# Attention's input norm computed beside the layer norm's own factor, and one product instead of two

## The chip, the cores and the metric

The kernel runs on one core of a Trainium2 chip. The metric is the device time of one execution in microseconds (us). A core has a matrix engine (TensorE, PE in the profile, with PEld for its weight loads), a vector engine (DVE), a scalar engine (ACT), GpSimd (POOL) and SyncE (SP), whose queue (SPq) issues the DMAs here. The engines run in parallel, each its own instructions in order, and meet only at semaphores.

## The reference, cut to what matters

The input is 2048 tokens of 128 channels. Six blocks follow one another, each behind a layer norm: mixture of experts, RWKV, mixture of experts, quantised feed-forward, attention of 16 heads of 64, quantised feed-forward. The change lies between the fourth block and the fifth:

```python
def _layernorm(x, axis=-1, eps=1e-05):
    m = jnp.mean(x, axis=axis, keepdims=True)
    v = jnp.var(x, axis=axis, keepdims=True)
    return (x - m) / jnp.sqrt(v + eps)

def rms_norm(x, gamma):                      # first step of the attention
    eps = 1e-12
    norm = jnp.maximum(jnp.linalg.norm(x, axis=-1, keepdims=True), eps)
    return x / norm * x.shape[-1] ** 0.5 * (gamma + 1.0)

x = x + _L1_attn_ref(_layernorm(x), ...)     # its input norm is rms_norm of the layer norm's output
```

With v the variance of a token, the layer norm's output has the length sqrt(128 v) / sqrt(v + eps). The second norm can so be had from v alone.

## The kernel before, in words

Everything stays on chip with channels on the 128 partitions and tokens along the free axis, in 4 chunks of 512 tokens (`NC`, `CH`), each of 4 tiles of 128 (`TPC`). The order of the work is written out by hand: each engine has a function for each block (`layer_norm`, `rms_norm`, `attention`, ...) and calls them one after another; semaphore counts tie the engines together. There are no planners and no pools.

A layer norm works so. PE multiplies x by a matrix of 1/128 (L575), which leaves the mean in PSUM; DVE subtracts it (L1179, into `late_cen`, which is a part of `p_raw`); ACT squares (L926). PE's `variances` (L559) multiplies each tile of squares by a column of 1/128, so that the variances of 128 tokens stand as a column, four columns a chunk. ACT takes the root of the 128x4 columns (L932, `ln_s`), DVE the reciprocal (L1184, `ln_r`). PE's `spread` (L566) takes each column, broadcast, as its weights and the identity as the other operand, which spreads the factor over all partitions. DVE multiplies the centred data by it (L1188, into `xn`, a part of `xnp`). PE runs these in the order variances 0 and 1, spread 0, variances 2, spread 1, variances 3, spread 2, spread 3.

`rms_norm` is then a second pass of the same form over `xn`: ACT squares it (L1009), PE sums (L559 again), ACT takes the root with scale 128 (L1012), DVE clamps at 1e-12 and inverts (L1355, L1356), PE spreads (L566), and DVE multiplies `xn` by the factor and by `gamma1`, which is (gamma + 1) times the root of 128 (L1360).

The attention begins with a prologue. ACT rounds `xn` to the matmul's format (L941, `x_h`), DVE takes the rest (L1194, `x_l`). When all four chunks of `x_l` are there PE projects queries and keys of heads 0 and 1 (L584 to L586, 24 matmuls) and the values of the first pair (L681 to L683). ACT and DVE evict the projections (L1032, L1371), and SP moves the pieces to where the scores want them, six DMAs a chunk and head (L352, L359). When those of head 0 have landed PE computes the scores of head 0 (L882), DVE takes their maxima (L1491), the maxima are turned and moved (L703, L1053, L328), and the main loop over 16 heads begins (L717, L718 scores, L695 next head's scores, L732 and L735 values, L1082 and L1085 exponentials, L490 their low parts on POOL).

In the weights of the prologue ACT's L1017 and L1021 and POOL's L501 and L506 make high and low parts; SP loads the second head's weights (L363) once POOL is done with the first.

Of the kernel before, what the change touches and what calls it, by code (L numbers as in the profile page):

```python
# [8 lines left out]
ACT = mybir.ActivationFunctionType  # L9
# [4 lines left out]
C = 128  # L14
T = 2048
CH = 512
NC = T // CH
NT = T // 128
TPC = CH // 128
# [9 lines left out]
RMS_EPS = 1e-12  # L29
# [38 lines left out]
def macaron_kernel(nc, a, out, g_scratch, l_scratch, r_scratch):  # L68
    ctx = ExitStack()
    with ctx:  # L70
        def sb(name, shape, dt=fp32, where=ctx):
            return where.enter_context(nc.sbuf_tensor(name, shape, dt))

        def sem(name):
            return ctx.enter_context(nc.semaphore(name))
# [4 lines left out]
        xn = xnp[:, 1:T + 1]  # L80
# [5 lines left out]
        ln_s = sb("ln_s", [128, NT])  # L86
        eps = sb("eps", [128, 1])
        ln_r = sb("ln_r", [128, NT])
        gamma1 = sb("gamma1", [C, 1])


# [76 lines left out]
        late_cen, late_sqr = low_half[:, 0:T], low_half[:, T:2 * T]  # L168
# [5 lines left out]
        ps = ctx.enter_context(nc.psum_tensor("ps", [128, 8, CH], fp32))  # L174
# [13 lines left out]
        ln_std, ln_rec, ln_bc, ln_out = sem("ln_std"), sem("ln_rec"), sem("ln_bc"), sem("ln_out")  # L188
# [8 lines left out]
        wkv_out, o_ps = sem("wkv_out"), sem("o_ps")  # L197
        f_ps, f_sigmoid, f_silu, f_prod, f_hi, f_lo, f_down = (
            sem("f_ps"), sem("f_sigmoid"), sem("f_silu"), sem("f_prod"), sem("f_hi"), sem("f_lo"), sem("f_down"))
        rms_sq, rms_sum, rms_std, rms_rec, rms_bc, rms_out = (  # L200
            sem("rms_sq"), sem("rms_sum"), sem("rms_std"), sem("rms_rec"), sem("rms_bc"), sem("rms_out"))
        qk_loaded = sem("qk_loaded")
        wv_loaded, wo_loaded = sem("wv_loaded"), sem("wo_loaded")
        qkw_hi, qkw_lo, vw_hi, vw_lo = sem("qkw_hi"), sem("qkw_lo"), sem("vw_hi"), sem("vw_lo")
# [18 lines left out]
        def chunk(c):  # L223
            return ds(c * CH, CH)
# [326 lines left out]
        def _(pe):  # L551
            mm = nc.tensor.matmul

            def variances(src_ready, count, done, c, sqr):

                pe.wait_ge(src_ready, count)
                for t in range(TPC):
                    tile = slice(c * CH + t * 128, c * CH + t * 128 + 128)
                    last = mm(ps[:, 4 + c, t:t + 1], sqr[:, tile], inv_c[:, 0:1], start=True, stop=True)  # L559
                last.then_inc(done, 1)  # L560

            def spread(src_ready, count, done, c):

                pe.wait_ge(src_ready, count)
                for t in range(TPC):
                    last = mm(ps[:, c, t * 128:t * 128 + 128],  # L566
                              ln_r[:, TPC * c + t:TPC * c + t + 1].to_broadcast([128, 128]), ident[:, :], start=True, stop=True)
                last.then_inc(done, 1)
# [90 lines left out]
                    down(c - 1)  # L659
                down(NC - 1)  # L660

            def rms_norm():
                for c in range(NC + 1):
                    if c < NC:
                        variances(rms_sq, c + 1, rms_sum, c, late_sqr)
                    if c > 0:
                        spread(rms_rec, c, rms_bc, c - 1)

            def project_qk(par, c, bank):

                w_hi_ = qk_h[par][:, :, :].rearrange("p a d -> p (a d)")
# [238 lines left out]
            layer_norm(3)  # L910
            quant_ffn(0, 3)
            layer_norm(4)
            rms_norm()
            attention()
            layer_norm(5)
            quant_ffn(1, 5)
# [3 lines left out]
        def _(act):  # L920
            af = nc.scalar.activation

            def layer_norm(k):
                for c in range(NC):
                    act.wait_ge(ln_cen, NC * k + c + 1)
                    af((sqr if k < 3 else late_sqr)[:, chunk(c)], (cen if k < 3 else late_cen)[:, chunk(c)],  # L926
                       ACT.Square).then_inc(ln_sq, 1)
                if k == 0:
                    act.wait_ge(const_ready, CONST)
                for c in range(NC):  # L930
                    act.wait_ge(ln_var, NC * k + c + 1)
                    af(ln_s[:, TPC * c:TPC * c + TPC], ps[:, 4 + c, 0:TPC], ACT.Sqrt, bias=eps[:, 0:1]).then_inc(ln_std, 1)  # L932

            def high_parts(j):

                for c in range(NC):
                    if j == 3:
                        act.wait_ge(rms_out, c + 1)
                    else:
                        act.wait_ge(ln_out, NC * (0, 2, 3, 0, 5)[j] + c + 1)  # L940
                    af(x_h[:, chunk(c)], xn[:, chunk(c)], ACT.Copy).then_inc(xh_done, 1)  # L941

            def split_weights():
# [49 lines left out]
            def quant_ffn(k):  # L993
                high_parts(2 * k + 2)
                for c in range(NC):
# [5 lines left out]
                    for ht in range(HT1):  # L1001
                        act.wait_ge(f_prod, PRIME + at * HT1 + ht + 1)
                        act.wait_ge(f_down, PRIME + at)
                        af(f_h[:, ht, :], f_hid[:, ht, :], ACT.Copy).then_inc(f_hi, 1)

            def rms_norm():
                for c in range(NC):
                    act.wait_ge(ln_out, NC * 4 + c + 1)
                    af(late_sqr[:, chunk(c)], xn[:, chunk(c)], ACT.Square).then_inc(rms_sq, 1)  # L1009
                for c in range(NC):  # L1010
                    act.wait_ge(rms_sum, c + 1)
                    af(ln_s[:, TPC * c:TPC * c + TPC], ps[:, 4 + c, 0:TPC], ACT.Sqrt, scale=float(C)).then_inc(rms_std, 1)  # L1012

            def high_qk_weights(par, head):

# [135 lines left out]
            layer_norm(3)  # L1151
            quant_ffn(0)
            layer_norm(4)
            rms_norm()
            attention()
            layer_norm(5)
            quant_ffn(1)
# [3 lines left out]
        def _(dve):  # L1161
# [7 lines left out]
            def step(ins):  # L1169

                steps[0] += 1
                ins.then_inc(dve_step, 1)
                dve.wait_ge(dve_step, steps[0])

            def layer_norm(k):
                centred = cen if k < 3 else late_cen
                for c in range(NC):
                    dve.wait_ge(ln_mean, NC * k + c + 1)
                    tt(centred[:, chunk(c)], x[:, chunk(c)], ps[:, c, :], ALU.subtract).then_inc(ln_cen, 1)  # L1179
                for c in range(NC + 1):  # L1180
                    if c < NC:
                        tiles = slice(TPC * c, TPC * c + TPC)
                        dve.wait_ge(ln_std, NC * k + c + 1)
                        nc.vector.reciprocal(ln_r[:, tiles], ln_s[:, tiles]).then_inc(ln_rec, 1)  # L1184
                    if c > 0:
                        dve.wait_ge(ln_bc, NC * k + c)
                        dve.wait_ge(ln_cen, NC * k + c)
                        tt(xn[:, chunk(c - 1)], centred[:, chunk(c - 1)], ps[:, c - 1, :], ALU.mult).then_inc(ln_out, 1)  # L1188

            def low_parts(j):  # L1190

# [136 lines left out]
            def quant_ffn(k):  # L1328
# [16 lines left out]
                    if c > 0:  # L1345
                        add_down(c - 1)
                add_down(NC - 1)

            def rms_norm():

                for c in range(NC + 1):
                    if c < NC:
                        tiles = slice(TPC * c, TPC * c + TPC)
                        dve.wait_ge(rms_std, c + 1)
                        step(ts(ln_s[:, tiles], ln_s[:, tiles], RMS_EPS, None, ALU.max))  # L1355
                        nc.vector.reciprocal(ln_r[:, tiles], ln_s[:, tiles]).then_inc(rms_rec, 1)  # L1356
                    if c > 0:
                        done = chunk(c - 1)
                        dve.wait_ge(rms_bc, c)
                        stt(xn[:, done], xn[:, done], gamma1[:, 0:1], ps[:, c - 1, :], ALU.mult, ALU.mult).then_inc(rms_out, 1)  # L1360

            def low_qk(head, par, n, bank, hi, lo, staged):

# [157 lines left out]
            step(ts(gamma1[:, :], gamma1[:, :], 1.0, float(C) ** 0.5, ALU.add, ALU.mult))  # L1521
            quant_ffn(0)
            layer_norm(4)
            rms_norm()
            attention()
            layer_norm(5)
            quant_ffn(1)
# [39 lines left out]
```

## Time and profile before

| | us |
|---|---|
| median of 3 runs | 2193.35 (2187.97 to 2199.1) |
| the profiled execution | 2188.44 |
| its span, first to last instruction | 2186.7 |
| PE busy in the span | 2024.6 (93%) |
| DVE busy | 1846.7 (84%) |
| ACT busy | 1524.8 (70%) |
| POOL busy | 1416.0 (65%) |
| mean granted clock of PE | 0.950 of full speed |

A busy share is an average over stages with different limits. The layer norm ahead of the attention and the second norm lie between 578.8 and 607.7 us, the prologue of the attention from there to 672 us, its main loop from 672 to about 2,136 us. In the rows below a time is counted from the start of the span, "[idle before <-releaser]" is how long the engine stood before that row and what ended it, and rows with xN are N instructions merged.

### The profile page before, as it was taken

The numbers are of one execution on the slowest core, as the hardware profiler recorded it, in microseconds if no ns is written. First come the engines' busy times: TensorE is split into PE (matmuls) and PEld (weight loads), VectorE is DVE, ScalarE is ACT, GpSimd is POOL, SyncE is SP. The second block draws the span as 40 slices with busy tenths as digits, with TensorE's granted clock in tenths as the row PEclk, the third lists the DMA queues.
The fourth block names the chain that finished last, engine by engine and source line by source line (L and its number), as shares of the span: only waits on it lengthen the run. The fifth ranks groups of instructions, "written<-read, shape, count | busy, mean of one in ns | idle before, by whom it ended". The sixth has DMA issues, their size and how long they took to land. (4 is left out here: it accounts for less than half of the span.)

```text
span 2186.7 us, 25774 instructions
## 1 busy us (share of the span) xinstructions
PE 2024.6 (93%) x8352; PEld 1443.5 (66%) x8352; DVE 1846.7 (84%) x1997; ACT 1524.8 (70%) x1877; POOL 1416.0 (65%) x660
## 2 busy tenths in 40 slices
PE   5999738999868999999999999999999999999887
PEld 4777527777645766767676676676667667666554
DVE  5888785887567899899889889989988998999785
ACT  4666425665425788788788778878878787887764
POOL 1000010000206899899999989989999998999882
PEclk7999857999878999999999999999999999999998
DMA  3310002110050123032130322303223131220000
GB/s 106 75 49 30 0 0 55 49 52 17 0 119 1 42 48 69 16 70 50 41 68 19 68 42 48 68 14 73 43 47 68 18 70 39 48 69 16 6 1 20
DMA packets 77272, 94.68 MB, mean 43 GB/s; under 512 B 31755, under 2 KB 35211, under 8 KB 76870
## 3 DMA queue, kind: packets, MB, share of 16 engines
q1 hardware_dynamic: 77142, 93.04, 18.6%
q8 instruction: 70, 1.15, 0.2%
q14 instruction: 60, 0.49, 0.1%
HBM read 41.11 MB, written 1.42 MB: 19 GB/s over the span
## 5 line engine op out<-in xcount | busy, mean ns | idle before, releaser
L490 POOL TENSOR_TENSOR p_l<-p_raw,p_h 128x1024 fp32r<-128x1024 f32 x512 | 1242.3, 2454 | 140.8 <-ACT p_h L1085 126.7
L1082 ACT ACTIVATE p_raw<-ps 128x1024 f32<-128x1024 f32 x512 | 567.2, 1108 | 234.7 <-PE ps L718 234.1
L1401 DVE TENSOR_REDUCE m_part<-ps 128x1 f32<-128x1024 f32 x480 | 584.5, 1218 | 125.0 <-PE ps L695 124.2
L1085 ACT ACTIVATE p_h<-ps 128x1024 fp32r<-128x1024 f32 x512 | 524.1, 1024 | 0.0
L717 PE MATMUL ps<-qa,ka 128*128 128x512 f32 x1024 | 444.8, 434 | 2.0 <-ACT m_t L1053 2.0
L718 PE MATMUL ps<-qb,kb 65*128 65x512 f32 x1024 | 408.5, 399 | 0.0
L732 PE MATMUL ps<-p_h,v_hl 128*128 128x512 f32 x1024 | 403.1, 394 | 2.3 <-POOL p_l L490 2.2
L1395 DVE TENSOR_REDUCE l_sum<-p_raw 128x128 f32<-128x1280 f32 x256 | 377.1, 1477 | 0.4
L695 PE MATMUL ps<-ka,qa 128*128 128x512 f32 x960 | 315.1, 409 | 12.7 <-DVE m_part L1401 12.3
L735 PE MATMUL ps<-p_l,v_hl 128*64 128x512 f32 x1024 | 320.8, 394 | 0.0
L1381 DVE TENSOR_REDUCE p_raw<-p_raw 128x128 f32<-128x1024 f32 x256 | 309.0, 1208 | 11.7 <-ACT p_raw L1082 11.7
L717 PEld LDWEIGHTS ps<-qa,ka 128*128 128x128 f32 x1024 | 194.8, 190 | 113.3 <-issue 72.4
L965 ACT ACTIVATE big<-ps,b 128x512 f32<-128x512 f32 x256 | 175.7, 690 | 116.3 <-PE ps L586 116.3
L732 PEld LDWEIGHTS ps<-p_h,v_hl 128*128 128x128 f32 x1024 | 193.3, 189 | 80.2 <-issue 4.6
L695 PEld LDWEIGHTS ps<-ka,qa 128*128 128x128 f32 x960 | 171.8, 190 | 91.5 <-DVE m_part L1401 58.9
L718 PEld LDWEIGHTS ps<-qb,kb 65*128 65x128 f32 x1024 | 194.8, 190 | 53.1 <-issue 16.1
L735 PEld LDWEIGHTS ps<-p_l,v_hl 128*64 128x64 f32 x1024 | 138.3, 135 | 71.3 <-issue 1.1
L1234 DVE TENSOR_TENSOR h_l<-big,h_h 128x512 fp32r<-128x512 f32 x256 | 165.6, 689 | 6.2
L465 POOL MEMSET p_raw<- 128x512 f32 x1 | 0.6, 566 | 246.9 <-DVE x L1248 246.9
L463 POOL TENSOR_TENSOR cen<-big 128x2048 f32<-128x2048 f32 x1 | 4.5, 4549 | 229.6 <-ACT big L983 229.6
L1254 DVE CAST h_h<-big 128x512 fp32r<-128x512 f32 x128 | 54.6, 427 | 66.4 <-ACT big L965 66.4
L584 PE MATMUL ps<-h_h,w_l 128*128 128x512 f32 x256 | 103.9, 406 | 0.4
(185 smaller groups left out, 2669.2 us busy)
## 6 DMA issues: line engine op xcount, KB each, us to landing
big<-g_scratch SPq DMA_DIRECT2D x64, 256.0 KB, 3.2
xnp<-r_scratch SPq DMA_DIRECT2D x59, 256.0 KB, 3.9
qa<-qk_hi SPq DMA_DIRECT2D x112, 128.0 KB, 2.3
ka<-qk_hi SPq DMA_DIRECT2D x56, 128.0 KB, 2.3
kb<-qk_hi SPq DMA_DIRECT2D x56, 128.0 KB, 2.3
ka<-xnp SPq DMA_DIRECT2D x28, 128.0 KB, 2.3
qb<-xnp SPq DMA_DIRECT2D x28, 128.0 KB, 2.4
ka<-qk_low SPq DMA_DIRECT2D x28, 128.0 KB, 3.6
```

The costliest lines, as they stand in the source:

```text
L490: nc.gpsimd.tensor_tensor(p_l[:, g % 4, :, :], slots(g), p_h[:, g % 4, :, :].bitcast(fp32), ALU.subtract).then_inc(pl_done, 1)
L695: last = mm(ps[:, 4 + b, :], qa[par][:, it * 128:it * 128 + 128], ka[par][:, chunk(2 * half + b)], start=True, stop=True)
L717: mm(st, ka[par][:, jt * 128:jt * 128 + 128], qa[par][:, ds(c * CH, CH)], start=True, stop=False)
L718: last = mm(st, kb[par][:, jt * 128:jt * 128 + 128], qb[par][:, ds(c * CH, CH)], start=False, stop=True)
L732: return mm(ps[:, bank, :], v_hl[:, par, 2 * g + j, :], p_h[:, g % 4, j, :], start=start, stop=stop)
L735: return mm(ps[0:DH, bank, :], v_hl[:, par, 2 * g + j, 0:DH], p_l[:, g % 4, j, :], start=False, stop=False)
L965: af(h_raw[:, u % 4, :], ps[:, u % 4, :], ACT.Relu, bias=b1[:, e, ht:ht + 1]).then_inc(h_relu, 1)
L1082: af(slots(g), s_t, ACT.Exp).then_inc(raw_done, 1)
L1085: af(p_h[:, g % 4, :, :], s_t, ACT.Exp).then_inc(ph_done, 1)
L1381: nc.vector.tensor_reduce(p_raw[:, ACC, cols, 0], p_raw[:, 0:ACC, cols, :].rearrange("p g n b -> p n g b"), AX.XY, ALU.add).then_inc(half_ ...
L1395: nc.vector.tensor_reduce(l_sum[:, cols], p_raw[:, ACC:GROUPS + 1, cols, :].rearrange("p g n b -> p n g b"), AX.XY, ALU.add).then_inc(all_ ...
L1401: nc.vector.tensor_reduce(m_part[:, it, half:half + 1], ps[:, 4:6, :].rearrange("p b n -> p (b n)"), AX.X, ALU.max).then_inc(s_max, 1)
```

## The change

The function `rms_norm` is gone on all three engines. ACT's `layer_norm`, for the fifth layer norm (k == 4) alone, takes a second root of the same variances, scaled by 128, into a new 128x16 tile `ln_n`. DVE's new `norm_factor` makes of the two columns one factor: r = 1/ln_s, n = ln_n r, n = max(n, 1e-12), n = 1/n, factor = r n, written to `ln_r`. Each of the first four waits for the one ahead of it through a semaphore. The layer norm's last product becomes a product with three operands, centred data, `gamma1` and the spread factor. ACT's rounding of `xn` waits for this product instead of for the second pass.

```diff
+        ln_n = sb("ln_n", [128, NT])
...
@@ tensor engine
-            def rms_norm():
-                for c in range(NC + 1):
-                    if c < NC:
-                        variances(rms_sq, c + 1, rms_sum, c, late_sqr)
-                    if c > 0:
-                        spread(rms_rec, c, rms_bc, c - 1)
...
@@ scalar engine
                 for c in range(NC):
                     act.wait_ge(ln_var, NC * k + c + 1)
                     af(ln_s[:, TPC * c:TPC * c + TPC], ps[:, 4 + c, 0:TPC], ACT.Sqrt, bias=eps[:, 0:1]).then_inc(ln_std, 1)
+                    if k == 4:
+                        af(ln_n[:, TPC * c:TPC * c + TPC], ps[:, 4 + c, 0:TPC], ACT.Sqrt, scale=float(C)).then_inc(rms_std, 1)
...
-                    if j == 3:
-                        act.wait_ge(rms_out, c + 1)
-                    else:
-                        act.wait_ge(ln_out, NC * (0, 2, 3, 0, 5)[j] + c + 1)
+                    act.wait_ge(ln_out, NC * (0, 2, 3, 4, 5)[j] + c + 1)
                     af(x_h[:, chunk(c)], xn[:, chunk(c)], ACT.Copy).then_inc(xh_done, 1)
...
-            def rms_norm():
-                for c in range(NC):
-                    act.wait_ge(ln_out, NC * 4 + c + 1)
-                    af(late_sqr[:, chunk(c)], xn[:, chunk(c)], ACT.Square).then_inc(rms_sq, 1)
-                for c in range(NC):
-                    act.wait_ge(rms_sum, c + 1)
-                    af(ln_s[:, TPC * c:TPC * c + TPC], ps[:, 4 + c, 0:TPC], ACT.Sqrt, scale=float(C)).then_inc(rms_std, 1)
...
@@ vector engine
+            def norm_factor(c, tiles):
+
+                factor, norm = ln_r[:, tiles], ln_n[:, tiles]
+                dve.wait_ge(rms_std, c + 1)
+                step(nc.vector.reciprocal(factor, ln_s[:, tiles]))
+                step(tt(norm, norm, factor, ALU.mult))
+                step(ts(norm, norm, RMS_EPS, None, ALU.max))
+                step(nc.vector.reciprocal(norm, norm))
+                tt(factor, factor, norm, ALU.mult).then_inc(ln_rec, 1)
...
                         dve.wait_ge(ln_std, NC * k + c + 1)
-                        nc.vector.reciprocal(ln_r[:, tiles], ln_s[:, tiles]).then_inc(ln_rec, 1)
+                        if k == 4:
+                            norm_factor(c, tiles)
+                        else:
+                            nc.vector.reciprocal(ln_r[:, tiles], ln_s[:, tiles]).then_inc(ln_rec, 1)
                     if c > 0:
                         dve.wait_ge(ln_bc, NC * k + c)
                         dve.wait_ge(ln_cen, NC * k + c)
-                        tt(xn[:, chunk(c - 1)], centred[:, chunk(c - 1)], ps[:, c - 1, :], ALU.mult).then_inc(ln_out, 1)
+                        if k == 4:
+                            stt(xn[:, chunk(c - 1)], centred[:, chunk(c - 1)], gamma1[:, 0:1], ps[:, c - 1, :],
+                                ALU.mult, ALU.mult).then_inc(ln_out, 1)
+                        else:
+                            tt(xn[:, chunk(c - 1)], centred[:, chunk(c - 1)], ps[:, c - 1, :], ALU.mult).then_inc(ln_out, 1)
...
-            def rms_norm():
-
-                for c in range(NC + 1):
-                    if c < NC:
-                        tiles = slice(TPC * c, TPC * c + TPC)
-                        dve.wait_ge(rms_std, c + 1)
-                        step(ts(ln_s[:, tiles], ln_s[:, tiles], RMS_EPS, None, ALU.max))
-                        nc.vector.reciprocal(ln_r[:, tiles], ln_s[:, tiles]).then_inc(rms_rec, 1)
-                    if c > 0:
-                        done = chunk(c - 1)
-                        dve.wait_ge(rms_bc, c)
-                        stt(xn[:, done], xn[:, done], gamma1[:, 0:1], ps[:, c - 1, :], ALU.mult, ALU.mult).then_inc(rms_out, 1)
```

DVE's instructions before, from the fifth layer norm's reciprocals to the low parts `x_l` (the products into `xnp` of L1188 are the layer norm's, those of L1360 the second norm's):

```order
525 L1184 RECIPROCAL ln_r<-ln_s 128x4 x2
526 L1188 TENSOR_TENSOR xnp<-p_raw,ps 128x512
529 L1184 RECIPROCAL ln_r<-ln_s 128x4
530 L1188 TENSOR_TENSOR xnp<-p_raw,ps 128x512 x2
531 L1355 TENSOR_SCALAR ln_s<-ln_s 128x4
532 L1356 RECIPROCAL ln_r<-ln_s 128x4
535 L1360 SCALAR_TENSOR_TENSOR xnp<-xnp,gamma,ps 128x512
539 L1355 TENSOR_SCALAR ln_s<-ln_s 128x4
540 L1356 RECIPROCAL ln_r<-ln_s 128x4
541 L1360 SCALAR_TENSOR_TENSOR xnp<-xnp,gamma,ps 128x512 x2
542 L1194 TENSOR_TENSOR x_l<-xnp,x_h 128x512 x4
```

And in the changed kernel, the same stretch (a middle chunk left out; the two blocks of five at its start are chunks 0 and 1):

```order
525 L1161 RECIPROCAL ln_r<-ln_s 128x4
526 L1162 TENSOR_TENSOR ln_n<-ln_n,ln_r 128x4
527 L1163 TENSOR_SCALAR ln_n<-ln_n 128x4
528 L1164 RECIPROCAL ln_n<-ln_n 128x4
529 L1165 TENSOR_TENSOR ln_r<-ln_r,ln_n 128x4
530 L1161 RECIPROCAL ln_r<-ln_s 128x4
535 L1184 SCALAR_TENSOR_TENSOR xnp<-p_raw,gamma,ps 128x512
546 L1165 TENSOR_TENSOR ln_r<-ln_r,ln_n 128x4
547 L1184 SCALAR_TENSOR_TENSOR xnp<-p_raw,gamma,ps 128x512 x2
548 L1193 TENSOR_TENSOR x_l<-xnp,x_h 128x512 x4
```

Each reciprocal of the layer norm has become five small instructions ahead of the spread that waits for them, and the second round of small instructions and products is gone.

PE before, from the means of the fifth layer norm to the first projection (32 matmuls of variances and 32 of spreads, in two rounds):

```order
1643 L575 MATMUL ps<-x,inv_c 128x512 x4
1644 L559 MATMUL ps<-inv_c,p_raw 128x1 x8
1645 L566 MATMUL ps<-ident,ln_r 128x128 x4
1646 L559 MATMUL ps<-inv_c,p_raw 128x1 x4
1647 L566 MATMUL ps<-ident,ln_r 128x128 x4
1648 L559 MATMUL ps<-inv_c,p_raw 128x1 x4
1649 L566 MATMUL ps<-ident,ln_r 128x128 x8
1650 L559 MATMUL ps<-inv_c,p_raw 128x1 x8
1651 L566 MATMUL ps<-ident,ln_r 128x128 x4
1655 L566 MATMUL ps<-ident,ln_r 128x128 x8
1656 L584 MATMUL ps<-x_h,qk_l 128x512
```

PE in the changed kernel:

```order
1647 L566 MATMUL ps<-ident,ln_r 128x128 x4
1648 L559 MATMUL ps<-inv_c,p_raw 128x1 x4
1649 L566 MATMUL ps<-ident,ln_r 128x128 x8
1650 L584 MATMUL ps<-x_h,qk_l 128x512
1651 L585 MATMUL ps<-x_h,qk_h 128x512
```

The first round is unchanged and the projections follow it directly.

## Rows read from the trace of the kernel before

**Rows 1.** The page's busy times and instruction counts over the span.
```profile
PE 2024.6 (93%) x8352; PEld 1443.5 (66%) x8352; DVE 1846.7 (84%) x1997; ACT 1524.8 (70%) x1877; POOL 1416.0 (65%) x660
```

**Rows 2.** Busy time by stretch; the columns are in the first line.
```profile
core 0: us, PE busy (x) PEld busy (x) DVE busy (x) ACT busy (x) POOL busy (x), PEclk, DMA share, GB/s
586.00:597.00 11.00, 10.77 (x53) 10.78 (x54) 3.39 (x8) 2.31 (x6) 0.00 (x0) 0.54 0.01 1
597.00:607.00 10.00, 9.86 (x60) 9.57 (x60) 3.79 (x13) 2.88 (x8) 0.00 (x0) 0.67 0.00 0
...
669.00:679.00 10.00, 7.92 (x20) 5.61 (x21) 1.23 (x1) 6.22 (x8) 2.67 (x2) 0.50 0.00 1
...
1044.00:2032.00 988.00, 978.55 (x4053) 676.82 (x4052) 902.14 (x844) 792.20 (x891) 926.19 (x418) 1.00 0.22 47
```

**Rows 3.** DVE in order of time, 586 to 611 us: start, length, instruction.
```profile
586.00 0.33 DVE L1184 RECIPROCAL ln_r<-ln_s 128x4 f32<-128x4 f32 x2 [2.27 <-ACT ln_s L932]
...
596.36 0.69 DVE L1188 TENSOR_TENSOR xnp<-p_raw,ps 128x512 f32<-128x512 f32 x1 [1.02 <-PE ps L566]
597.81 0.17 DVE L1355 TENSOR_SCALAR ln_s<-ln_s 128x4 f32<-128x4 f32 x1 [0.76 <-ACT ln_s L1012]
598.01 0.18 DVE L1356 RECIPROCAL ln_r<-ln_s 128x4 f32<-128x4 f32 x1
...
606.90 0.75 DVE L1360 SCALAR_TENSOR_TENSOR xnp<-xnp,gamma,ps 128x512 f32<-128x512 f32 x1 [0.96 <-PE ps L566]
607.57 3.01 DVE L1194 TENSOR_TENSOR x_l<-xnp,x_h 128x512 fp32r<-128x512 f32 x4
```

**Rows 4.** PE in order of time, 586 to 612 us.
```profile
586.23 1.56 PE L566 MATMUL ps<-ident,ln_r 128*128 128x128 f32 x8 [1.55 <-DVE ln_r L1184]
587.58 1.71 PE L559 MATMUL ps<-inv_c,p_raw 128*128 128x1 f32 x8
589.15 2.05 PE L566 MATMUL ps<-ident,ln_r 128*128 128x128 f32 x8
591.00 1.71 PE L559 MATMUL ps<-inv_c,p_raw 128*128 128x1 f32 x8
592.56 3.76 PE L566 MATMUL ps<-ident,ln_r 128*128 128x128 f32 x16
...
610.63 0.74 PE L584 MATMUL ps<-x_h,qk_l 128*128 128x512 f32 x1 [3.76 <-DVE x_l L1194]
```

**Rows 5.** ACT in order of time, 585 to 608 us.
```profile
585.70 0.42 ACT L932 ACTIVATE ln_s<-ps,eps 128x4 f32<-128x4 f32 x2
...
592.74 0.26 ACT L932 ACTIVATE ln_s<-ps,eps 128x4 f32<-128x4 f32 x1 [3.15 <-PE ps L559]
...
607.68 0.63 ACT L941 ACTIVATE x_h<-xnp 128x512 fp32r<-128x512 f32 x1 [1.08 <-DVE xnp L1360]
```

**Rows 6.** DVE, dependent small instructions of the first block, near 43 us.
```profile
43.28 0.25 DVE L1222 RECIPROCAL rt<-rt 128x16 f32<-128x16 f32 x1
43.57 0.18 DVE L1223 TENSOR_TENSOR rt<-rt 128x16 f32<-128x16 f32 x1
43.78 0.29 DVE L1224 TENSOR_TENSOR best<-best,rt 128x128 f32<-128x128 f32 x1
```

**Rows 7.** The prologue in order of time: ACT, POOL, SP's queue, PE.
```profile
611.76 0.46 POOL L501 TENSOR_TENSOR qk_l<-qk_raw,qk_h 128x128 fp32r<-128x128 f32 x1 [1.74 <-ACT qk_h L1017]
...
612.97 1.15 SPq L352 DMA_DIRECT2D qa<-p_raw  x2
...
628.58 0.60 SPq L359 DMA_DIRECT2D qb<-p_raw  x1
...
631.05 3.72 PE L882 MATMUL ps<-ka,qa 128*128 128x512 f32 x8 [7.71 <-DMA qb<-p_raw]
```

**Rows 8.** PE, last layer norm (2147 us) and start of the main loop (from 672 us).
```profile
2147.94 1.16 PE L566 MATMUL ps<-ident,ln_r 128*128 128x128 f32 x8 [1.55 <-DVE ln_r L1184]
2148.93 0.95 PE L559 MATMUL ps<-inv_c,p_raw 128*128 128x1 f32 x8
...
673.11 0.63 PE L717 MATMUL ps<-qa,ka 128*128 128x512 f32 x1
673.54 0.63 PE L718 MATMUL ps<-qb,kb 65*128 65x512 f32 x1
...
679.05 0.40 PE L717 MATMUL ps<-qa,ka 128*128 128x512 f32 x1
679.28 0.39 PE L718 MATMUL ps<-qb,kb 65*128 65x512 f32 x1
```

More of the change, by code:

```diff
@@ L199, in macaron_kernel @@
             sem("f_ps"), sem("f_sigmoid"), sem("f_silu"), sem("f_prod"), sem("f_hi"), sem("f_lo"), sem("f_down"))
-        rms_sq, rms_sum, rms_std, rms_rec, rms_bc, rms_out = (
-            sem("rms_sq"), sem("rms_sum"), sem("rms_std"), sem("rms_rec"), sem("rms_bc"), sem("rms_out"))
+        rms_std = sem("rms_std")
         qk_loaded = sem("qk_loaded")
@@ L912, in _ @@
             layer_norm(4)
-            rms_norm()
             attention()
@@ L1153, in _ @@
             layer_norm(4)
-            rms_norm()
             attention()
@@ L1523, in _ @@
             layer_norm(4)
-            rms_norm()
             attention()
```

## The prediction

> **What bounds the kernel now.** I read the page first for the shares over the whole span. PE is busy 93% of it and is the nearest thing to a bound [rows 1]. The busy times by stretch say where that holds: in the middle of the attention PE is busy 978.55 of 988 us at the full granted clock, while the change leaves not one instruction of this loop different [rows 2]. The change lies in the 29 us ahead of the attention's prologue, so what counts is the chain of single waits there, and I read each engine in order of time. Two facts are to be seen. First, in the layer norm from 586.23 us on, PE runs without a gap from spread 0 to spread 3 (each row of PE starts before the one above it has ended) at a granted clock of 0.54, which is nearly all at the lower level of 1.2 GHz: there PE is the bound, and ACT's roots and DVE's reciprocals lie beside its work [rows 2, 4]. Second, nothing of the attention starts before the last low part is written: PE stands for 3.76 us until `x_l` at 610.63 [rows 4]. The second norm is thus wholly on the path that sets the end: it is the time between the layer norm's last product, begun at 596.36, and its own last product, begun at 606.90 [rows 3]. Behind either the same work follows: rounding, low parts, projections.
>
> **What goes.** 606.90 - 596.36 = 10.54 us on the path. In it are 16 matmuls of variances and 16 of spreads, 4 squares and 4 roots on ACT, 8 small instructions and 4 products on DVE. Half of the second pass ran at the higher clock level (granted clock 0.67 for 597 to 607 [rows 2]), so this price is from a mixture of both.
>
> **What comes.** On ACT a second root of the same columns behind each first. Two such roots together take 0.42 us against 0.26 for one, so the second ends 0.16 us after the first one's issue plus its own length; the roots of the second norm were shorter, about 0.17, and I let DVE start 0.07 us later than before [rows 5]. On DVE the one reciprocal of a chunk becomes five dependent instructions on 128x4. In the second norm the clamp and the reciprocal, tied by the same kind of wait, start 0.20 us apart [rows 3]; in the first block a dependent reciprocal takes 0.29 and a dependent product 0.21 to the next start, on 16 columns [rows 6]. I take 0.20 for each of the four added steps: 0.80 us for the first chunk. PE waited for exactly this chunk (1.55 us of idle in front of spread 0 [rows 4]), so spread 0 starts 0.87 us later, at 587.10.
>
> The other three chunks: does PE still cover them? I shift PE's rows by 0.87. Variances 2 end at 590.16; the roots take until 590.5, the factor until 591.5; it is needed at spread 2, which PE reaches at 593.43, so there are 1.9 us to spare. Chunk 1's factor is ready at 588.1 for a spread at 590.0. Chunk 3 is the tight one: variances 3 end at 593.58, roots at 593.9, factor at 594.95. Spread 3 comes half-way through the row of 16 and is reached at 592.56 + 0.87 + 1.88 = 595.31, and its weight load (which is what reads the factor) some 0.3 us ahead of that [rows 4]. That is cover of about nil: I charge 0.05. DVE's in-order queue adds nothing, since each product stands behind a factor that is finished before the product's own spread (chunk 2's product waits for a spread that ends at 595.3, the factor of chunk 3 in front of it is done at 594.95). The new product has three operands and 0.75 us instead of 0.69, but the product that is now last replaces one of the same kind, so nothing is added.
>
> **Sum.** The last product starts at 596.36 + 0.87 + 0.05 = 597.28 instead of 606.90: 9.6 us gained. The bounds of the step price, from the rows: 0.155 (two independent reciprocals take 0.33 with 0.18 for one [rows 3]) to 0.32 (the dependent product on 128 columns with its 0.29). At 0.155 the gain is 9.8; at 0.32 the first chunk costs 1.35 and chunk 3 comes 0.45 later against its cover, which makes 8.7. If no chunk were covered, four times 0.87 would be paid, and 7.1 us remain.
>
> For a small DVE instruction on SBUF the Trainium skill (Perfetto Trace Analysis, Optimizing Scalar/DVE Operations) names about 60 ns of engine time, twice that as profiled latency. By 60 ns for each of the four steps the gain would be 10.2 instead of 9.6; the trace has 0.20 from start to start where the next one waits, and I go by that.
>
> **What is late next, and is it moved rigidly?** Everything behind the last product hangs on it. ACT's fourth rounding began at 607.68, right behind the last product [rows 5]; now the first three are done earlier still, and the fourth keeps its place. The low parts take 3.01 us from there [rows 3]. The second head's weights are ready at 612.22 [rows 7], 1.6 us after the first projection; they hang on ACT's instructions right behind the roundings, so they move along. From then SP paces the prologue: its first move is issued at 612.97, the 24th at 628.58, and PE waits 7.71 us for it to land [rows 7]; the projections have already ended then. Then DVE's maxima pace it. Neither has changed. No DMA, no table load and no instruction of the loop is added or taken away. So I pass the 9.6 us on in full.
>
> Against the profiled execution: span 2186.7 - 9.6 = 2177.1, plus 1.7 around it, 2178.8 us. This execution is 4.9 us under the median shown, near the lowest of the runs; from the median the same gain gives 2183.7. The changed kernel will be read as a median of runs like those, so I take 2183.
>
> **The rivals.**
> The clock, for the better. The layer norm's tail ran at the lower level. At the higher one eight spreads take 1.16 us instead of about 2 and eight variances 0.95 instead of 1.71 [rows 4, 8]. If the changed kernel has the higher level from 587 on, PE reaches the end of variances 3 at 590.6, the roots and the factor of chunk 3 follow uncovered until 591.95, spread 3 takes 1 us: last product at 593.1, 4.2 us more, gain 13.8, 2179 us. For it: the level changes several times in this region (0.54, 0.67, 0.50 [rows 2]). Against: up to 586 us both kernels do the same, and PE now has a longer wait before spread 0, no shorter one.
>
> The gain is partly given back. The prologue and the first groups of the main loop run behind PE's waits, and there a matmul at the lower level comes every 0.43 us instead of every 0.23 [rows 8]; the stretch of 669 to 679 is at 0.50 throughout [rows 2]. If the shift puts one more such 10 us on a stretch where PE paces, 23 matmuls cost 0.2 us more each, 4.6 us in all; gain 5, 2188 us. For it: PE's 7.7 us wait for the moves and the level after it. Against: the waits ahead of all these stretches have the same length as before.
>
> The Trainium skill (TensorE: Matmul & The Clock Gate, Part 1) says that the clock is either half or full, falls when PE idles and comes back after it has worked, and that the moment depends on a schedule that runs free of the kernel, so that the count of slow matmuls differs from run to run; it puts the penalty below 1% of a typical span. By this rule the two rivals above are luck of either sign rather than effects of the change; the trace agrees so far that 0.50 follows a wait of PE each time it is seen.
>
> Slower. The clock in the main loop: PE is busy 99% there, so it has nothing to hide a lower level behind. 9.6 / 0.2 = 48 more matmuls of 512 columns at the lower level eat the gain, and to be 11 us slower than before it takes 103, a stretch of some 45 us. At, say, 110 it would be 2205 us. For it: no wait in the loop would have to be long, a drift between engines might do. Against: 1.00 over 988 us, and a loop whose instructions and waits stay as they are.
>
> That the change doesn't do what it says can be left out: PE's order shows 32 of its 64 matmuls here gone.
>
> **How the numbers follow.** What a measurement of this kernel can tell from no change is about 0.5%, 11 us; 9.6 us is 0.44%, just under it. The forecast has 0.66 (its own range 2176 to 2191: gain 7 to 12 with the scatter of the runs), the better clock 0.14, partly given back 0.16, the slower one 0.04. The three runs of before lie 11 us apart, so of the forecast's 0.66 a third, 0.22, is measured beyond 11 us. Faster by over 0.5%: 0.22 + 0.14 = 0.36. Within: 0.44 + 0.16 = 0.60. Slower: 0.04. The range of 8 in 10 leaves out the last case and the ends of the others: 2173 to 2193.
>
> **What would show it.** The first spread of this layer norm at 587.1 instead of 586.2, with DVE's five small instructions 0.20 us apart in front of it; PE without a gap from there to spread 3, or a gap of under 0.3 us before it; the last product near 597.3; the first projection near 601.0 instead of 610.63, the first scores near 621.5 instead of 631.05, the start of the main loop near 662.5 instead of 672.1. Wrong if one of the later three has moved by other than 9 to 10 us, if small dependent instructions come slower than 0.3 us apart, or if the loop's length differs.

## The result, and the profile after

| | before | changed |
|---|---|---|
| median (lowest to highest), 7 runs each | 2189.74 (2186.33 to 2199.1) | 2173.6 (2166.9 to 2179.51) |
| profiled execution / its span | 2188.44 / 2186.7 | 2179.51 / 2177.7 |

The ratio of the changed kernel to the one before is 0.9918 with a 95% interval of 0.9889 to 0.9948: 18 us faster, 11 to 24 (the medians lie 16 us apart). Forecast were 9.6 us, and 0.60 went to a difference that a measurement of this kernel can't tell from none; the interval excludes that there is none. Two more measurements of the same kernel, beside other kernels on other occasions, gave 0.9927 (0.9905 to 0.9949) and 0.9930 (0.9905 to 0.9956).

I read first where the forecast had put its marks. ACT's first two roots of the changed layer norm (they answer to [rows 5]):

```profile
578.89 0.26 ACT L924 ACTIVATE ln_s<-ps,eps 128x4 f32<-128x4 f32 x1
579.05 0.16 ACT L926 ACTIVATE ln_n<-ps 128x4 f32<-128x4 f32 x1
```

DVE behind them, in order of time (it answers to [rows 3]):

```profile
579.32 0.18 DVE L1161 RECIPROCAL ln_r<-ln_s 128x4 f32<-128x4 f32 x1 [2.40 <-ACT ln_n L926]
579.53 0.16 DVE L1162 TENSOR_TENSOR ln_n<-ln_n,ln_r 128x4 f32<-128x4 f32 x1
579.73 0.17 DVE L1163 TENSOR_SCALAR ln_n<-ln_n 128x4 f32<-128x4 f32 x1
579.93 0.18 DVE L1164 RECIPROCAL ln_n<-ln_n 128x4 f32<-128x4 f32 x1
580.15 0.16 DVE L1165 TENSOR_TENSOR ln_r<-ln_r,ln_n 128x4 f32<-128x4 f32 x1
...
587.69 0.18 DVE L1161 RECIPROCAL ln_r<-ln_s 128x4 f32<-128x4 f32 x1 [1.18 <-ACT ln_n L926]
...
588.52 0.16 DVE L1165 TENSOR_TENSOR ln_r<-ln_r,ln_n 128x4 f32<-128x4 f32 x1
...
590.89 0.75 DVE L1184 SCALAR_TENSOR_TENSOR xnp<-p_raw,gamma,ps 128x512 f32<-128x512 f32 x1 [0.96 <-PE ps L566]
```

PE in the same stretch and at the two marks behind it (it answers to [rows 4, 7, 8]):

```profile
580.36 1.95 PE L566 MATMUL ps<-ident,ln_r 128*128 128x128 f32 x8 [2.49 <-DVE ln_r L1165]
582.11 1.71 PE L559 MATMUL ps<-inv_c,p_raw 128*128 128x1 f32 x8
583.67 2.06 PE L566 MATMUL ps<-ident,ln_r 128*128 128x128 f32 x8
585.52 1.71 PE L559 MATMUL ps<-inv_c,p_raw 128*128 128x1 f32 x8
587.09 3.76 PE L566 MATMUL ps<-ident,ln_r 128*128 128x128 f32 x16
594.62 0.79 PE L584 MATMUL ps<-x_h,qk_l 128*128 128x512 f32 x1 [3.77 <-DVE x_l L1193]
...
614.17 2.04 PE L875 MATMUL ps<-ka,qa 128*128 128x512 f32 x4 [7.04 <-DMA qb<-p_raw]
...
655.47 0.80 PE L710 MATMUL ps<-qa,ka 128*128 128x512 f32 x1 [2.02 <-ACT m_t L1036]
```

The five small instructions, of which each of the last four waits for the one before it, come 0.20 to 0.22 us apart. Spread 0 follows 0.21 us behind the last of them, and from there PE runs without a gap to spread 3. The last product starts 10.5 us after spread 0 (10.1 before), the projections behind it. But all of this lies 6 to 7 us earlier in the span than it should: spread 0 at 580.36 where 587.10 was forecast, the first projection at 594.62 for 601.0, the first scores at 614.17 for 621.5, the main loop at 655.47 for 662.5. The last three have moved by 16 to 17 us, where the forecast called itself wrong for anything but 9 to 10. The gain has a part ahead of the change. So I cut the span at marks that both kernels have, DVE's first subtraction of each layer norm. The first layer norm's comes at 6.22 us before and 6.21 in the changed kernel; the four rows that follow are the second to the fifth layer norm, which end the first expert block, RWKV, the second expert block and the quantised block. The kernel before, then the changed one:

```profile
233.41 1.87 DVE L1179 TENSOR_TENSOR cen<-x,ps 128x512 f32<-128x512 f32 x3
...
315.65 1.47 DVE L1179 TENSOR_TENSOR cen<-x,ps 128x512 f32<-128x512 f32 x2
...
535.79 2.47 DVE L1179 TENSOR_TENSOR p_raw<-x,ps 128x512 f32<-128x512 f32 x4
...
580.46 0.69 DVE L1179 TENSOR_TENSOR p_raw<-x,ps 128x512 f32<-128x512 f32 x1 [0.72 <-PE ps L575]
```

```profile
229.54 2.47 DVE L1171 TENSOR_TENSOR cen<-x,ps 128x512 f32<-128x512 f32 x4
...
310.86 1.32 DVE L1171 TENSOR_TENSOR cen<-x,ps 128x512 f32<-128x512 f32 x2
...
525.86 2.47 DVE L1171 TENSOR_TENSOR p_raw<-x,ps 128x512 f32<-128x512 f32 x4
...
573.44 0.69 DVE L1171 TENSOR_TENSOR p_raw<-x,ps 128x512 f32<-128x512 f32 x1 [1.02 <-PE ps L575]
```

| stage | before | changed | difference |
|---|---|---|---|
| first expert block (first layer norm to second) | 227.19 | 223.33 | -3.86 |
| RWKV | 82.24 | 81.32 | -0.92 |
| second expert block | 220.14 | 215.00 | -5.14 |
| first quantised block | 44.67 | 47.58 | +2.91 |
| changed norm, up to the first projection | 30.17 | 21.18 | -8.99 |
| from there to the main loop | 61.47 | 60.85 | -0.62 |
| main loop to the end | 1514.6 | 1522.2 | +7.6 |

The expert blocks, in which the change alters not one instruction, are 9 us faster. The page's groups for PE between 55 and 90 us, inside the first chunk of the first expert block, before and after:

```profile
L584 PE MATMUL ps<-x_h,w_l 128*128 128x512 f32 x26 | 10.3, 396 | 0.0
L586 PE MATMUL ps<-h_l,w_h 128*128 128x512 f32 x26 | 10.3, 395 | 0.0
L584 PE MATMUL ps<-h_h,w_l 128*128 128x512 f32 x25 | 10.0, 399 | 0.0
```

```profile
L586 PE MATMUL ps<-h_l,w_h 128*128 128x512 f32 x26 | 10.1, 390 | 0.0
L584 PE MATMUL ps<-x_h,w_l 128*128 128x512 f32 x26 | 10.1, 389 | 0.0
L584 PE MATMUL ps<-h_h,w_l 128*128 128x512 f32 x26 | 10.1, 389 | 0.0
```

And PE's work in that stretch, first before, then changed (columns as in [rows 2]):

```profile
55.00:90.00 35.00, 35.00 (x152) 28.27 (x151) 28.26 (x49) 24.00 (x40) 0.00 (x0) 1.00 0.44 93
```

```profile
55.00:90.00 35.00, 35.00 (x156) 28.96 (x155) 28.99 (x50) 24.70 (x40) 0.00 (x0) 1.00 0.35 93
```

The same 35 us, all at full granted clock and PE busy throughout, hold 156 matmuls instead of 152. Below, "cadence" is the mean distance of the starts of two successive 512-column matmuls, over the pairs 0.205 to 0.25 us apart; for the first expert block, from 110 to 215 us, these are some 440. It is 232.5 ns before and 227.1 ns in the changed kernel, in the second expert block 232.4 and 227.4; in the main loop 232.4 and 232.6 (other windows move such a mean by 0.1 or 0.2 ns). The share of the DMA engines, which differs between the two kernels from 55 to 90 us, is 0.13 and 0.14 from 110 to 215 us, so it is not what makes the difference there.

### The profile page after: what moved, and what is told of

Its sections match the earlier page's. It is cut to its first block and busy times, and to the rows that moved or that the text cites. A ratio compares the mean times of both kernels' runs of the same rounds, so it can differ in the third digit from the quotient of the medians.

```text
span 2177.7 us, 25650 instructions
## 1 busy us (share of the span) xinstructions
PE 2010.9 (92%) x8288; PEld 1438.4 (66%) x8288; DVE 1852.0 (85%) x2001; ACT 1521.1 (70%) x1873; POOL 1414.8 (65%) x660
## 5 line engine op out<-in xcount | busy, mean ns | idle before, releaser
L463 POOL TENSOR_TENSOR cen<-big 128x2048 f32<-128x2048 f32 x1 | 4.5, 4530 | 227.0 <-ACT big L974 227.0
```

## The experiments

What in the change can reach a block that it doesn't touch? It adds a tile, `ln_n`, of 64 bytes a partition, in front of `gamma1`. All tiles allocated behind it lie 64 bytes higher, among them the experts' weights `w1_h` to `w2_l` and the hidden tiles `h_h`, `h_l`; `x_h` and `x_l` lie in front of it and stay. My theory A was this place in SBUF, the memory on the chip that holds all tiles; the rivals were B, the shorter program, and C, luck of the runs. Below, two tiles are "in step" when their starts lie a multiple of 128 bytes apart within a partition. In the kernel before, the weights and the hidden tiles lie 64 bytes off from `x_h`; with the 64 bytes of `ln_n` in front of them all are in step.

**The place without the norm.** The kernel before, with an unused tile:

```diff
         ln_r = sb("ln_r", [128, NT])
+        spare = sb("spare", [128, NT])
         gamma1 = sb("gamma1", [C, 1])
```

> The kernel before with one unused tile of 64 bytes a partition put where the change puts ln_n; the instructions are the same as before, every tile from gamma1 on lies 64 bytes higher. Theory A (the part of the gain that I did not forecast comes from where the tiles lie in SBUF): the matmuls of the two expert blocks follow one another every 0.227 us instead of 0.233, 8 to 10 us faster than before, ratio about 0.996. Theory B (it comes from the shorter program or its place in memory): ratio 1.000, cadence 0.233. Theory C (it was luck of the runs compared): ratio 1.000, and the cadence is either one by chance.

Measured: cadence 227.2 in the first expert block and 227.2 in the second; ratio 0.9987 (0.9963 to 1.0012). The cadence is as theory A has it with the program of before, so B falls for the expert blocks; C, by which one profile's cadence may be chance, falls with the ten profiles of the table below. The end-to-end time showed less than the forecast 8 to 10 us.

**The norm without the place.** The changed kernel with

```diff
-        ln_n = sb("ln_n", [128, NT])
...
         r_col = sb("r_col", [128, 2, TPC], where=two)
+        ln_n = sb("ln_n", [128, NT], where=two)
```

> The changed kernel with ln_n allocated behind all other tiles, so that every other tile lies where it lay before. Theory A: only the forecast gain is left, 9 to 10 us, ratio about 0.9956, cadence of the expert blocks 0.233. Theory B: as the changed kernel, 16 to 19 us, ratio about 0.992, cadence 0.227. Theory C: 9 to 10 us, with the cadence by chance.

Measured: ratio 0.9967 (0.9949 to 0.9985), cadence 232.5 and 232.6. The norm alone gives 7.2 us (3 to 11), and the 9.6 forecast for it lie within that.

**Other distances.** 32 unused bytes in the kernel before (`sb("spare", [128, 8])` in the same place), and 32 more in the changed kernel behind `ln_n`.

> The kernel before with an unused tile of 32 bytes in the same place: the weights and the attention's tiles then start on a multiple of 128 bytes. Theory A with alignment as its cause: the expert blocks at 0.227 or less, and perhaps the main loop of the attention (0.2325 in both kernels) faster too, which would be up to 30 us. Theories B and C: ratio 1.000.

Measured: 1.0005 (0.9981 to 1.0029), cadence 231.3 and 231.4; main loop 232.4. Being on a multiple of 128 is not what counts, and the loop doesn't respond.

> The changed kernel with 32 more unused bytes behind ln_n (shift of 96 in all against before; tiles on a multiple of 64 but not of 128). Theory A: 9.6 us from the change and besides whatever this place gives; if only the offset from a multiple of 64 counts, as e3. Theory B: as the changed kernel, 16 to 19 us under before.

Measured: 0.9964 (0.9947 to 0.9981), cadence 230.8 and 231.3. With 32 bytes more the changed kernel is level with the norm alone (0.9967): about half of its gain is gone.

**Both halves once more, and all tiles together.** Four kernels side by side: the changed one, the norm alone, the 64 bytes alone, and the changed one with

```diff
+        spare = sb("spare", [128, 24])
         x = sb("x", [C, T])
```

> The changed kernel once more, beside the next three on one chip. If the norm gives 9.6 us and the place of the tiles the rest: ratio 0.992 to 0.993 (15 to 18 us), cadence of the expert blocks 0.227. If its first measurement was partly luck: ratio near 0.9956.

Measured: 0.9927 (0.9905 to 0.9949), cadence 226.9 and 227.0.

> The changed kernel with ln_n behind all other tiles (all others as before), again. If the norm alone gives what the chain of waits says: 9 to 10 us, ratio 0.9956, and 5 to 9 us slower than the changed kernel beside it. Rival, that the norm gives 16 us by itself: ratio 0.992, level with the changed kernel.

Measured: 0.9956 (0.9940 to 0.9973), cadence 232.5 and 232.4. The norm is worth 9.6 us here, and the changed kernel beside it is faster by another 0.3%, though the two intervals still overlap from 0.9940 to 0.9949.

> The kernel before with 64 unused bytes in front of gamma1, again. If the faster cadence of the expert blocks (0.0061 us on each of 2 x 768 matmuls, 9 us) reaches the end: ratio 0.996. If it is absorbed by waits for other engines or by the clock: ratio 0.999 to 1.000, as its first measurement (0.9987) had it.

Measured: 0.9984 (0.9965 to 1.0002), cadence 227.1 and 227.2.

> The changed kernel with 96 unused bytes in front of x, so that x_h and x_l move along and every tile keeps its distance to them. If the distance between weights and moving data counts: cadence 0.227 and time as the changed kernel. If the absolute place counts (fast only 32 bytes behind a multiple of 128): cadence 0.231 to 0.233, and 5 to 9 us slower than the changed kernel.

Measured: 0.9918 (0.9895 to 0.9941), cadence 227.1 and 227.2. PE's groups of this kernel, 55 to 90 us:

```profile
L585 PE MATMUL ps<-x_h,w_l 128*128 128x512 f32 x27 | 10.5, 389 | 0.0
L586 PE MATMUL ps<-x_h,w_h 128*128 128x512 f32 x27 | 10.5, 389 | 0.0
```

With `x_h` moved along, no tile's address is what it was (the weights start on a multiple of 128 now, 32 bytes behind one in the changed kernel), and the fast cadence stays. It is the distance between the tiles that counts, not where each lies.

**Which tiles.** The norm-alone kernel with 64 bytes more in front of `w1_h` and 192 in front of `h_h` (weights in step with `x_h`, hidden tiles not), and the same with 64 in front of `h_h` alone:

```diff
+        spare = sb("spare", [128, 16], where=one)
         w1_h = sb("w1_h", [C, E, H0], fp32r, one)
...
+        spare2 = sb("spare2", [128, 48], where=one)
         h_h = sb("h_h", [128, 4, CH], fp32r, one)
```

> The changed kernel with every tile where it lay before, but the experts' weights 64 bytes higher, in step with x_h and x_l (distance a multiple of 128 bytes), the hidden tiles h_h and h_l out of step. If the distance between weights and x_h counts: cadence of the first products near 0.227. If it is x_h against h_h: 0.233. If all three must be in step: between 0.229 and 0.233.

Measured: cadence 231.7 and 231.7; one time, 2183.03.

> The same with only h_h and h_l 64 bytes higher, in step with x_h, the weights as before. If the distance between the moving tiles x_h and h_h counts: cadence 0.227. If the weights' place counts: 0.233.

Measured: cadence 229.0 and 229.1; one time, 2175.6. Each alone gives a part (0.8 and 3.5 ns), both together 5.4 ns. So the fast cadence wants `x_h`, the weights and the hidden tiles in step. Whether these three are enough is not shown: `cen`, `sqr` and `big`, which other engines use in this block, moved in every kernel with 5.4 ns and in neither of these two, and in the first of the two the tiles between the weights and `h_h` (`b1` to `rt`) moved with the weights.

| distance of weights / hidden tiles from `x_h`, bytes over a multiple of 128 | kernels | cadence, first block, ns |
|---|---|---|
| 64 / 64 | before, norm alone (twice) | 232.5 |
| 96 / 96 | 32 bytes, old norm | 231.3 |
| 32 / 32 | changed, 32 bytes more | 230.8 |
| 0 / 64 | weights up | 231.7 |
| 64 / 0 | hidden tiles up | 229.0 |
| 0 / 0 | ten profiles: changed, 64 bytes alone, all up 96 and their variants | 226.9 to 227.2 |

**Is it a rule for the attention as well?** Its projection weights lie 32 bytes out of step with `x_h` in the changed kernel:

```diff
-        qk_scale = sb("qk_scale", [128, 1], where=two)
...
         r_col = sb("r_col", [128, 2, TPC], where=two)
+        qk_scale = sb("qk_scale", [128, 1], where=two)
```

> The changed kernel with the 32-byte tile qk_scale moved behind all others, so that the attention's projection weights, wv_hl and l_sum are in step with x_h and inv_c as well (multiples of 128 bytes apart; 32 bytes off before). If being in step is what makes matmuls follow at 0.227: the projections L584 to L586 of the attention go from 0.2324 on average to 0.227, 24 in the prologue and 168 in the loop with their value projections, 1 to 2 us in all, ratio 0.0005 to 0.001 lower than the changed kernel's 0.9927. If not: no change in their cadence or the time.

Measured: ratio 0.9888 (0.9868 to 0.9907). But the matmul behind each of the loop's projections follows at 232.6, 232.5 and 229.9 ns (`x_h` with the low part of the weights, `x_h` with the high part, `x_l` with the high part), on average 231.7 against 233.8, 233.6 and 233.8 in the three profiles of the changed kernel: some 2 ns less, and not the 227 expected. 168 of them in the loop make 0.4 us. The trace shows no stage that is faster by more than its scatter. So I ran it again beside the changed kernel.

> The changed kernel with qk_scale behind all other tiles, again, beside the changed kernel on one chip. By its trace no stage is over 1 us faster than in the changed kernel, so ratio 0.992 to 0.993 and level with it; if its 0.9888 was an effect of this place, 6 to 9 us faster than the changed kernel beside it.

Measured: 0.9905 (0.9883 to 0.9927).

> The changed kernel a third time, as the reference for the run before this one: ratio 0.992 to 0.993.

Measured: 0.9930 (0.9905 to 0.9956). The medians of these two lie 7 us apart (2171.68 and 2178.78), yet the intervals overlap; the lowest runs are equal (2166.33 and 2166.28). The kernel with `qk_scale` moved is the fastest measured, against the one before without doubt; that it beats the changed one is likely and not shown.

**The place alone, once more,** now with the old norm and both moves:

> The kernel before with the 64 unused bytes and qk_scale behind all others: the place of the tiles as in the first of this call, the second norm as before. If the place is worth the same with and without the new norm: 9 to 10 us slower than the first. The two measurements of the 64 bytes alone gave 0.9987 and 0.9984, their difference to the norm-alone runs says 0.997: this run tells which.

Measured: 0.9970 (0.9953 to 0.9987), cadence 227.0 and 227.1. Against the kernel with the same places and the new norm, measured beside it (0.9905), this is 13 us (2185.11 and 2171.68), more than the 9 to 10 expected but within what the two intervals leave open.

**The cover of the last chunk.** The changed kernel with the clamp written five times:

```diff
                 step(ts(norm, norm, RMS_EPS, None, ALU.max))
+                step(ts(norm, norm, RMS_EPS, None, ALU.max))
+                step(ts(norm, norm, RMS_EPS, None, ALU.max))
+                step(ts(norm, norm, RMS_EPS, None, ALU.max))
+                step(ts(norm, norm, RMS_EPS, None, ALU.max))
```

> The changed kernel with the clamp of the factor written five times instead of once, so four more dependent small DVE instructions a chunk (the values stay the same). By the working of the forecast each costs 0.20 us; the first chunk's 0.8 are on the path and so are the last one's, since its cover is nil: from the first subtraction of this layer norm to the first projection 1.6 us more than the 20.8 to 21.2 of the changed kernel, 22.4 to 22.8. If PE still covered the later chunks 21.6 to 22.0; if no chunk were covered 24.0 or more.

Measured: from the first subtraction of this layer norm to the first projection 22.86 us. Eleven profiles with the new norm have 20.77 to 21.25, mean 21.05. PE in this kernel:

```profile
590.72 2.05 PE L566 MATMUL ps<-ident,ln_r 128*128 128x128 f32 x8
593.18 2.08 PE L566 MATMUL ps<-ident,ln_r 128*128 128x128 f32 x8 [0.41 <-DVE ln_r L1169]
```

Spread 2 and spread 3 are now two rows with a gap that ends by DVE's factor. 1.8 us more than 21.05: the first chunk's 0.81 and about as much for the last. The cover was nil, as the working had it. This kernel ran once; its time, 2177.78, says nothing about so small a cost, the stretch in its profile does.

## Why the prediction was wrong

The range held the time (2173 to 2193 against 2173.6), but at its edge and by luck: its lower end stood there for the scatter and for a better clock, and the expert blocks, which brought the time there, were in neither. The likeliest case (2176 to 2191) and its 9.6 us did not hold. Of the 9.4 us between the forecast 2183 and the measured 2173.6, 3.6 are the starting point alone: the median of before was 2193.35 of three runs and is 2189.74 of seven.

**What went and what came: right.** 10.54 us out in this profile, 0.20 us for each added step, spread 0 later by the first chunk's four steps, chunks 1 and 2 covered, chunk 3 on the edge. The stretch from the first subtraction to the first projection was forecast as 20.5 us. Eleven profiles with the new norm have 21.05 on average, five with the old one 31.1 (30.17 to 33.10). So the step is worth 10.1 us. The profile of before was 1 us on the lucky side of its own average: its second norm took 10.54 us from last product to last product, in the other four 10.56, 11.32, 11.38 and 13.65, by how much of it ran at the higher clock level. (That was a third of the time in the profile of before, granted clock 0.67, and not the half that the forecast named.) In the changed one DVE starts 0.43 us behind the first root (579.32 - 578.89) where I had 0.37, and spread 0 takes 1.75 us to the next row instead of 1.35, because the granted clock falls to its lower level 0.17 us after its start instead of 0.59 (0.67 from 580.3 to 581.0, 0.95 from 586.2 to 586.9 before). End to end, the norm alone measures 0.9956 and 0.9967: 9.6 and 7.2 us.

**"Is it moved rigidly?": wrong.** The sentence that failed is "No DMA, no table load and no instruction of the loop is added or taken away. So I pass the 9.6 us on in full." I took unchanged instructions for unchanged durations, and asked what lies behind the change in time, never what lies behind the new tile in memory. What failed is thus the term for the stages ahead of the change, which the forecast put at nothing without a reason. What the runs show in its place: the two expert blocks got faster, by 5.4 ns on each of 2 x 768 matmuls, 8.3 us. From mark to mark the two blocks together take 447.3, 442.7 and 442.8 us in the three profiles with the old places (before, and the norm alone twice), and 432.6 to 441.1, mean 438.1, in the ten profiles with everything in step: 6.2 us less. With the 9.6 of the norm this makes 16 to 18 us, and the three measurements of the changed kernel stand at 15 to 18.

Behind the change the shift was rigid from the first scores to the main loop (41.3 us against 41.05), but not ahead of that: 614.17 - 594.62 = 19.55 us from first projection to first scores, 20.42 before. This isn't scatter: the twelve profiles with the new norm have 19.55 to 19.61, the five with the old one 20.27 to 20.98, 1.1 us more on average. The forecast's "Neither has changed" for what paces the prologue is so not right: in each of the five one of SP's 24 issues, the 8th to the 10th, takes 1.35 to 2.05 us instead of 0.60, and one packet of 16 KB of the instruction queue starts in this stretch (at 618.04 in the profile of before); in none of the twelve is there either. The slow issue before, with the instruction queue's traffic from 616 to 620 us (packets, MB, share of the DMA engines), and the same issue in the changed kernel:

```profile
618.02 1.56 SPq L352 DMA_DIRECT2D ka<-p_raw  x1
q8 instruction: 1, 0.02, 1.8%
```

```profile
602.05 0.60 SPq L352 DMA_DIRECT2D ka<-p_raw  x1
```

That the packet makes the issue wait is likely and not shown, and why the packet comes there with the old norm alone is open. Up to the main loop the new norm is so worth 11.1 us (92.9 to 81.8, means of the five and of eleven profiles), a little more than the 9.6 and 7.2 of the two end-to-end measurements.

One thing is not settled by this. The 64 bytes alone measured 0.9987, 0.9984 and, with `qk_scale` moved too, 0.9970: 3 to 7 us, each interval 4 to 5 us to either side. Their mean is nearer to 4 than to the 8.3 us of the cadence. What absorbs the rest in these runs, or whether it is scatter, is open. So the cadence is shown to come from the place of the tiles, and that it is the part of the gain that was not forecast follows from the sum; its worth end to end is known only as 3 to 8 us.

**The rivals.** The better clock in this norm's tail did not come: here are the busy times of the changed kernel (columns as in [rows 2]), with its norm in the first and the middle of its main loop in the second row. The 0.61 has 1.5 us at full clock ahead of spread 0 in it; from there PE's rows have the lengths of before (1.71, 2.06, 1.71 and 3.76 us against 1.71, 2.05, 1.71 and 3.76):

```profile
579.00:586.00 7.00, 5.64 (x27) 5.64 (x28) 3.44 (x17) 0.77 (x6) 0.00 (x0) 0.61 0.01 2
...
1034.00:2022.00 988.00, 978.75 (x4053) 677.65 (x4052) 902.22 (x846) 790.96 (x888) 925.10 (x417) 1.00 0.22 46
```

"Partly given back", with its 5 us of gain, did not come either, but a smaller loss can't be excluded. The main loop, from its first scores to the last ones, took 1444.3 us in the profile of before and 1450.8 in the changed kernel's; but the loops of all 17 profiles lie between 1444.3 and 1456.8, those of the other four kernels with the old norm between 1446.4 and 1451.7. It was the profile of before that was short. On average the loop takes 1449.0 us in the five with the old norm and 1451.2 in the twelve with the new one, 2 us more, where single profiles scatter by 3. That 0.50 follows a wait of PE "each time it is seen" is not so: PE works without a gap from 586.23 on [rows 4], and the granted clock, back at 1.00 from 597.1, falls to 0.50 again at 600.5. Slower: no sign of it, the loop is at 1.00 here as well.

The one pair of traces shows 9.0 us in the span where the medians show 16: 2.9 us in the quantised block and 7.6 from the main loop's start on stand against it. Both are scatter: the quantised block takes 44.6 to 47.6 us in the 17 profiles, and 44.65 in another profile of the changed kernel. The cut by stages, not the total, showed the cause.

**The chances.** 0.66 for the likeliest case was not too high by its own steps. What was missing is a case for what a new tile does to the others, of either sign.

## What to carry to other kernels

A change that allocates a tile also moves every tile behind it. Print the addresses of both kernels before forecasting, and to measure the idea by itself put the new tile behind all others. When a stage that no instruction of the change touches has another duration, compare mean durations of the same instruction between the traces: 396 against 389 ns gave it away.

## What the runs showed of the hardware

In the expert blocks, at a granted clock of 1.00, back-to-back 512-column matmuls in the rounded format (fp32r) follow one another at 226.9 to 227.4 ns when the weights and both moving tiles start a multiple of 128 bytes apart within a partition (and the tiles allocated beside them have moved along), and at 229.0 to 232.6 ns when one or both are 32, 64 or 96 bytes off, with the same instructions. Moving all tiles together by 96 bytes changed nothing (227.1). The main loop of the attention stayed at 232.4 to 232.7 ns in all kernels, although its tiles are in step with one another in all of them; being in step is so not enough there. Why is open, as is what in the memory or in the engines makes the difference.

Dependent DVE instructions on 128x4 start 0.20 to 0.22 us apart whatever they are (product, clamp, reciprocal), in chains of five and of nine.
